# First output tile on one Trainium2 core: products with the low weights behind those with the high ones, and VectorE's three low parts behind the last head's P

## The chip, the cores and the metric

The kernel runs on one core of a Trainium2 chip. The metric is the device time of one execution in microseconds (us); of several executions the median counts. A comparison is called same when it lies within 0.2% (2.8 us here).

## The reference

The input x has 8 rows (batches) of 512 tokens with 1024 values, all float32. Two blocks follow each other:

```
x = x + layernorm(attention(layernorm(x)))      # 8 heads of 64, w_qkv (1536 x 1024), w_o (1024 x 512)
x = x + layernorm(ffn(layernorm(x)))            # W (1024 x 1024), b, and a low-rank part:
ffn(h) = h @ W.T + b + (h @ A[:r].T) @ B[:, :r].T   # r of 8, 16, 32, 64, chosen per token by the gate's largest score
attention: scores = k q^T, masked scores -10000, softmax over the key axis, times v, then w_o
```

## The kernel before

**Products in three passes.** Every float32 product is made of three TensorE products: an operand is split into a high part (rounded to the fast float32 form) and a low part (the rest), and high x high, high x low and low x high are added in PSUM. ScalarE makes the high parts (an ACTIVATE with Copy), VectorE or GpSimd the low parts (a subtraction of the high part from the raw one). For the FFN the weights W, A and the gate lie side by side in `wag`, 8 chunks (k = 0 to 7) of 128 x 1092: raw `wag_raw`, high `wagh`, low `wagl`. The activations are `x2Th` and `x2Tl`.

**Two phases.** `attention_phase` walks over the 8 rows of x: projections, then for each of 8 heads (h) the scores, their softmax `pr` (the P of a head; GpSimd normalises it in `normalise`, four tensor_scalar over 512, 384, 256 and 128 columns), the transposes of P into `ps_t` in three groups g = 0, 1, 2 (`transpose_p`), high and low parts of the transposed P (`p_hi` on ScalarE, `p_lo` on VectorE) and the values (`values`). `output_phase` walks over 32 tiles of 128 tokens: output product, layernorm, FFN (`ffn`), layernorm. Between them stands `last_body`, the attention of row 7, in which every engine's order is written out by hand: it already loads and splits the output phase's weights (`next_high`, `next_low`) and carries the first tiles through their output product (`tile_out` copies its PSUM halves out), residual (`tile_residual`), layernorm (`tile_scale`, `tile_norm`, `tile_statistics`) and transposes (`tile_high`, `tile_low`: the high and low parts of x2 of tile 0).

**What sets the order.** Each engine runs its own queue in order. Between engines there are only counting semaphores, waited for with `wait_ge`. Those that matter here: `next_lo` counts VectorE's low parts (three of w_o, then wag[4], wag[5], wag[6], so 4, 5, 6 of the table `LOW_READY` plus one mean these), `next_lo_pool` those of GpSimd (w_o 3, wag[0] to wag[3], wag[7]); `x2_lo` counts the halves of `tile_low`; `us_ready` tells that the routing of tile 0 (`route` on VectorE) is done, after which TensorE transposes `us`.

**The first FFN tile.** `ffn` makes three PSUM banks in the order 2, 0, 1. Per bank and chunk k it issues high x high, high x low weight, low x high weight. Into the first bank of tile 0 it puts the rest of the attention phase: after k = 1 `last_transposes` (the third group of the last head's P) and after k = 4 `last_values` (the last head's values).

```python
LOW_READY = {4: KV, 5: KV + 1, 6: KV + 2}

next_low(W.wag[4])        # VectorE, last_body
next_low(W.wag[5])
tile_low()
p_lo(7, 0, b)
p_lo(7, 1, b)
vals_sum(6, b)
p_lo(7, 2, b)
next_low(W.wag[6])
product_statistics(2)
vals_sum(7, b)
tile_statistics(1)
```

GpSimd's own end of `last_body`, which the change leaves as it is, reads: weights and normalise of head 7, diagonal, `tile_scale(0, 1, 1)`, `next_low(W.wag[7])`, `tile_residual(1)` (two additions of 128 x 512), `tile_scale(1, 4, 1)`, `tile_scale(0, 2, 2)`.

Of the kernel before, what the change touches and what calls it, by code (L numbers as in the profile page):

```python
# [33 lines left out]
class Output:  # L34
# [3 lines left out]
    def __init__(self, nc, ctx, whole, S, D, PART, R, NAG):  # L38
        def sb(name, shape, dt, c=ctx):
            return c.enter_context(nc.sbuf_tensor(name, shape, dt))  # L40

        def sem(name):
            return whole.enter_context(nc.semaphore(name))

        KD, KV = D // P, PART // P
        self.R, self.KV = R, KV

        self.woh = sb("woh", [P, KV, D], F32R)
        with ExitStack() as early:
            wo_raw = sb("wo_raw", [P, KV, D], F32, early)  # L50
        self.wol = sb("wol", [P, KV, D], F32R)
        self.vraw = sb("vraw", [P, 2, KV, P], F32)
        self.vh = sb("vh", [P, 2, KV, P], F32R)
        self.vl = sb("vl", [P, 2, KV, P], F32R)

        self.wagh = sb("wagh", [P, KD, NAG], F32R)
        self.bo_s = sb("bo_s", [P, D], F32)
        with ExitStack() as early:
            wag_raw = sb("wag_raw", [P, KD, NAG], F32, early)
            B_raw = sb("B_raw", [P, D], F32, early)  # L60
        self.wagl = sb("wagl", [P, KD, NAG], F32R)
        self.Bl = sb("Bl", [P, D], F32R)
        self.Bh = sb("Bh", [P, D], F32R)
        self.y = [sb(f"y{i}", [P, D], F32) for i in range(3)]
        used = 2 * KD * NAG + 2 * D + D + 3 * D
        small = sb("small", [P, 2 * KD * (2 * PART + S) - used - P], F32)
        self.uT = sb("uT", [P, P], F32R)

        with ExitStack() as early:
            self.z = sb("z", [P, D], F32, early)  # L70
            self.xs = [sb("xt0", [P, D], F32, early)]
        self.plane4 = [sb("plane4h", [P, 2, PART], F32R), sb("plane4l", [P, 2, PART], F32R)]
        self.spare = small[:, 128:128 + PART]
        self.stats_2 = small[:, 72:84]

        self.x1 = [sb("x1_0", [P, D], F32), self.y[0]]
        self.x2Th = [sb("x2Th0", [P, KD, P], F32R)]
        self.x2Tl = [sb("x2Tl0", [P, KD, P], F32R)]
        self.x2n = sb("x2n", [P, D], F32)
        self.floats = 2 * KV * D + 6 * PART + 2 * KD * (2 * PART + S) + 6 * D  # L80

        self.stats = [small[:, 12 * c:12 * c + 12] for c in range(3)]
        row = [[36 + 5 * i + j for j in range(5)] for i in range(6)]
        self.mv = [small[:, r[0]:r[0] + 2] for r in row]
        self.var_eps = [small[:, r[2]:r[2] + 1] for r in row]
        self.rstd = [small[:, r[3]:r[3] + 1] for r in row]
        self.shift = [small[:, r[4]:r[4] + 1] for r in row]
        self.gb_s = small[:, 66:70]

        self.chunks = [("wo", k, wo_raw[:, k, :], self.woh[:, k, :], self.wol[:, k, :]) for k in range(KV)]  # L90
        self.chunks += [("wag", k, wag_raw[:, k, :], self.wagh[:, k, :], self.wagl[:, k, :]) for k in range(KD)]
        self.chunks += [("B", 0, B_raw[:, :], self.Bh[:, :], self.Bl[:, :])]
        self.wag, self.B = range(KV, KV + KD), KV + KD

        self.next_lo = sem("next_lo")
        self.next_lo_pool = sem("next_lo_pool")
        self.bo_landed = sem("bo_landed")
        self.gb_landed = sem("gb_landed")
        self.v_landed = [sem(f"v_landed{i}") for i in range(2)]
        self.x_landed = [sem(f"xt_landed{i}") for i in range(2)]  # L100
        self.v_hi = sem("v_hi")
        self.v_ready = sem("v_ready")
        self.o_full = sem("o_full")
        self.y_done = sem("y_done")
        self.mv_ready = [sem(f"mv_ready{i}") for i in range(3)]
        self.ln_ready = [sem(f"ln_ready{i}") for i in range(3)]
        self.z_done = sem("z_done")
        self.x1_done = sem("x1_done")
        self.x2n_ready = sem("x2n_ready")
        self.x2_full = sem("x2_full")  # L110
        self.x2_hi = sem("x2_hi")
        self.x2_lo = sem("x2_lo")
        self.zf_done = sem("zf_done")
        self.out_done = sem("out_done")
        self.f_done = sem("f_done")
        self.out_stored = [sem(f"out_stored{i}") for i in range(2)]
        self.m_full = sem("m_full")
        self.m_out = sem("m_out")
# [7 lines left out]
def attention_phase(nc, whole, x, wqkvT, bqk, bv, valsT, wl_late, vals_stored, ps_o, C, W, woT, bo, wagT, BT, gb):  # L126
# [58 lines left out]
    with ExitStack() as ctx:  # L185
# [3 lines left out]
        def sem(name):  # L189
            return whole.enter_context(nc.semaphore(name))  # L190
# [109 lines left out]
        vlo_done = sem("vlo_done")  # L300
        vals_ready = sem("vals_ready")
        next_landed = [sem(f"next_landed{n}") for n in range(len(W.chunks))]
        next_hi = sem("next_hi")
        next_lo, next_lo_pool = W.next_lo, W.next_lo_pool

        HIGH_ROWS = [PT[:, PT_OFF[j]:PT_OFF[j] + (NT - j) * P] for j in range(NT)]
# [383 lines left out]
        def vector(dve):  # L690
# [243 lines left out]
            def last_body(b):  # L934
# [47 lines left out]
                tile_out(0, 1)  # L982
                p_lo(4, 0, b)
                p_lo(4, 1, b)
                vals_sum(3, b)
                reciprocal(5, b)
                tile_vals_low(2)
                p_lo(4, 2, b)

                scores_max(6, b)  # L990
                tile_out(1, 0)
# [15 lines left out]
                p_lo(6, 2, b)  # L1007
                reciprocal(7, b)

                next_low(W.wag[4])  # L1010
                next_low(W.wag[5])
                tile_low()
                p_lo(7, 0, b)
                p_lo(7, 1, b)
                vals_sum(6, b)
                p_lo(7, 2, b)
                next_low(W.wag[6])
                product_statistics(2)
                vals_sum(7, b)
# [675 lines left out]
def output_phase(nc, whole, x, valsT, vals_stored, ps_o, C, W, woT, bf, out):  # L1695
# [19 lines left out]
    with ExitStack() as ctx:  # L1715
# [3 lines left out]
        def sem(name):  # L1719
            return whole.enter_context(nc.semaphore(name))  # L1720
# [597 lines left out]
        def tensor(pe, last_transposes, last_values):  # L2318
# [74 lines left out]
            def low_rank(banks):  # L2393
                for g in banks:
# [3 lines left out]
                                         stop=(Bp is Bl), skip_group_check=True)  # L2398
                    last.then_inc(f_full, 1)

            def ffn(b, i, last_tiles, first_tiles):
                first = first_tiles and i == 0
                n = 4 * b + i
                xh, xl = x2Th[i % 2], x2Tl[i % 2]
                pe.wait_ge(x2_lo, 2 * n + 2)
                pe.wait_ge(next_lo_pool, 5)
                for m, g in enumerate(BANK_ORDER):
                    cols = slice(GW * g, GW * g + GW)

                    pe.wait_ge(f_done, 3 * n + m + 1)  # L2410
                    for k in range(KD):
                        if m == 0 and k in LOW_READY:
                            pe.wait_ge(next_lo, LOW_READY[k])
                        elif m == 0 and k == KD - 1:
                            pe.wait_ge(next_lo_pool, 6)
                        for a, w in ((xh, wagh), (xh, wagl), (xl, wagh)):
                            last = pe.matmul(ps_f[:, g, 0:GW], a[:, k, :], w[:, k, cols],  # L2417
                                             start=(k == 0 and a is xh and w is wagh), stop=False,
                                             skip_group_check=True)
                        if first and g == 2 and k == 1:  # L2420
                            last_transposes(pe)
                        if first and g == 2 and k == KD // 2:
                            last_values(pe)
                        if g == 1 and k == (0 if last_tiles else KD - 3):

                            pe.wait_ge(us_ready, n + 1)
                            if not first_tiles:
                                pe.wait_ge(m_out, 7 * pair_count(b, 0 if last_tiles else i) + (11 if i % 2 and not last_tiles else 7))
                            pe.transpose(ps_u[:, 0:P].bitcast(F32R), us[:, :].bitcast(F32R), ident_r[:, :])\
                                .then_inc(ut_full, 1)  # L2430
                            if not last_tiles:
                                transpose_x2(n + 1)
                        if g == 1 and k == KD // 2 - 1 and last_tiles:

                            pe.wait_ge(ut_ready, n + 1)
                            low_rank(BANK_ORDER[:2])
                    if g == 2:
                        last.then_inc(u_full, 1)
                        if i % 2 and not first_tiles and not last_tiles:
                            pair_third(b, i)  # L2440
                    if g == 0 and last_tiles and i < 3:
                        transpose_x2(n + 1)

                if last_tiles:
                    low_rank(BANK_ORDER[2:])
                else:
                    pe.wait_ge(ut_ready, n + 1)
                    pe.wait_ge(next_lo, KV + 3)
                    low_rank(BANK_ORDER)
# [86 lines left out]
```

## Time and profile before

| | us |
|---|---|
| median of 3 executions | 1416.1 (1415.28 to 1416.1) |
| the profiled execution | 1415.63 |
| its span (first to last instruction) | 1413.8 |
| TensorE busy | 1396.7 |
| VectorE busy | 1045.6 |
| GpSimd busy | 709.0 |
| ScalarE busy | 693.3 |

The profiled execution took 1.83 us more than its span; that part lies outside of the instructions. In the rows PE is TensorE, DVE VectorE, ACT ScalarE, POOL GpSimd. Matmuls overlap, so TensorE's pace is read from the distance of their starts, not from their durations. The end of attention and the first FFN tile lie between 800 and 850 us of the span.

### The profile page before, as it was taken

The numbers are of one execution on the slowest core, as the hardware profiler recorded it, in microseconds if no ns is written. First come the engines' busy times: TensorE is split into PE (matmuls) and PEld (weight loads), VectorE is DVE, ScalarE is ACT, GpSimd is POOL, SyncE is SP. The second block draws the span as 40 slices with busy tenths as digits, with TensorE's granted clock in tenths as the row PEclk, the third lists the DMA queues.
The fourth block names the chain that finished last, engine by engine and source line by source line (L and its number), as shares of the span: only waits on it lengthen the run. The fifth ranks groups of instructions, "written<-read, shape, count | busy, mean of one in ns | idle before, by whom it ended". The sixth has DMA issues, their size and how long they took to land.

```text
span 1413.8 us, 25005 instructions
## 1 busy us (share of the span) xinstructions
PE 1396.7 (99%) x7796; PEld 1249.2 (88%) x7796; DVE 1045.6 (74%) x2204; ACT 693.3 (49%) x1498; POOL 709.0 (50%) x1268
## 2 busy tenths in 40 slices
PE   7999999999999999999999999999999999999998
PEld 6888888888888888888888889999999999999998
DVE  7676685776775776766756888898878787878764
ACT  6365465564573664654654863433333333333332
POOL 3364462572562563644624785555555555555542
PEclk9999999999999999999999999999999999999999
DMA  7334334224233243342332643232222222222311
GB/s 253 127 98 121 113 93 148 89 97 139 97 111 108 94 139 111 96 122 111 95 102 93 213 145 109 105 105 92 102 89 104 104 103 89 91 92 99 119 75 60
DMA packets 68773, 157.54 MB, mean 111 GB/s; under 512 B 7424, under 2 KB 31232, under 8 KB 68736
## 3 DMA queue, kind: packets, MB, share of 16 engines
q1 hardware_dynamic: 68736, 157.08, 33.3%
q8 instruction: 19, 0.31, 0.1%
q14 instruction: 18, 0.15, 0.0%
HBM read 62.15 MB, written 25.69 MB: 62 GB/s over the span
## 4 chain that ended last, share of the span: by engine, by line
PE 89%; POOL 4%; issue 3%; POOLq 1%; DVE 1%; ACT 1%; DVEq 1%; DMA 0%; SPq 0%; ACTq 0%
PE ps_f L2417 23%; PE ps_o L1483 21%; PE ps_o L1514 12%; PE ps_s L1534 6%; PE ps_o L2336 6%; PE ps_v L1358 5%; PE ps_t L1396 3%; PE ps_o L1477 3%; PE ps_z L2336 2%; PE ps_f L2397 2%; PE ps_o L1437 2%; PE ps_x L2387 1%; PE ps_v L1366 1%; POOL wagl L609 1%; PE ps_o L1495 1%
## 5 line engine op out<-in xcount | busy, mean ns | idle before, releaser
L2417 PE MATMUL ps_f<-wagh,x2Th 128*128 128x364 f32 x768 | 254.7, 332 | 0.0
L2417 PE MATMUL ps_f<-wagh,x2Tl 128*128 128x364 f32 x768 | 252.5, 329 | 0.0
L2417 PE MATMUL ps_f<-wagl,x2Th 128*128 128x364 f32 x768 | 252.1, 328 | 0.0
L1483 PE MATMUL ps_o<-xTh,wh 128*128 128x512 f32 x424 | 172.2, 406 | 0.0
L572 POOL TENSOR_SCALAR pr<-pr,nwm,rden 128x512 f32<-128x512 f32 (+3 forms) x256 | 161.0, 644 | 11.3 <-issue 11.3
L1483 PE MATMUL ps_o<-xTh,wl 128*128 128x512 f32 x424 | 166.1, 392 | 0.0
L1483 PE MATMUL ps_o<-xTl,wh 128*128 128x512 f32 x424 | 165.4, 390 | 0.0
L548 POOL TENSOR_TENSOR cw<-wm,cnt 128x4 f32<-128x4 f32 x64 | 12.8, 201 | 301.1 <-ACT pr L1122 301.1
L2417 PEld LDWEIGHTS ps_f<-wagh,x2Th 128*128 128x128 f32 x768 | 144.2, 188 | 1.9 <-DVE f L2117 0.2
L2417 PEld LDWEIGHTS ps_f<-wagl,x2Th 128*128 128x128 f32 x768 | 144.5, 188 | 1.6
L2417 PEld LDWEIGHTS ps_f<-wagh,x2Tl 128*128 128x128 f32 x768 | 144.4, 188 | 0.0
L724 DVE TENSOR_TENSOR PT<-ps_t,PT 128x512 fp32r<-128x512 f32 (+1 forms) x192 | 110.5, 598 | 36.8 <-ACT PT L1079 32.5
L1122 ACT ACTIVATE pr<-ps_s,nm 128x128 f32<-128x128 f32 (+3 forms) x256 | 131.0, 524 | 0.2
L1079 ACT ACTIVATE PT<-ps_t 128x512 fp32r<-128x512 f32 (+1 forms) x192 | 95.2, 530 | 57.2 <-PE ps_t L1396 50.6
L1881 POOL TENSOR_TENSOR small<-small,eps 128x1 f32<-128x1 f32 x90 | 20.9, 232 | 198.8 <-DVE small L1961 184.3
L786 DVE TENSOR_REDUCE nm<-ps_s 128x1 f32<-128x129 f32 (+3 forms) x256 | 108.0, 484 | 2.2
L1514 PE MATMUL ps_o<-wh_v,xTh 128*128 128x512 f32 x256 | 100.5, 393 | 0.0
L1514 PE MATMUL ps_o<-wh_v,xTl 128*128 128x512 f32 x256 | 99.8, 390 | 0.0
L1483 PEld LDWEIGHTS ps_o<-xTh,wl 128*128 128x128 f32 x424 | 79.6, 188 | 17.9
L1534 PE MATMUL ps_s<-kst,qst 128*128 128x128 f32 (+3 forms) x512 | 94.2, 326 | 0.0
L2207 ACT ACTIVATE f<-f,small 128x512 f32<-128x512 f32 x62 | 47.2, 809 | 95.2 <-POOL small L1885 95.2
L1358 PEld LDWEIGHTS ps_v<-PT,v 128*128 128x128 f32 x512 | 83.5, 188 | 9.6 <-issue 1.4
(303 smaller groups left out, 3425.4 us busy)
## 6 DMA issues: line engine op xcount, KB each, us to landing
p_words<-pr SPq DMA_DIRECT2D x56, 448.0 KB, 2.8
kst<-kst SPq DMA_DIRECT2D x64, 256.0 KB, 3.7
x<-in_x SPq DMA_DIRECT2D x31, 512.0 KB, 3.4
x2r<-x2n SPq DMA_DIRECT2D x30, 512.0 KB, 2.9
xs<-in_x SPq DMA_DIRECT2D x24, 512.0 KB, 4.4
out<-x SPq DMA_DIRECT2D x23, 512.0 KB, 2.6
p_words<-pr SPq DMA_DIRECT2D x56, 192.0 KB, 2.3
valsT<-vt SPq DMA_DIRECT2D x64, 128.0 KB, 2.3
```

The costliest lines, as they stand in the source:

```text
L572: done = pool.tensor_scalar(at, at, nwm[:, q, i:i + 1], rden[:, q, i:i + 1], ALU.add, ALU.mult)
L724: dve.tensor_tensor(LOW_GROUPS[g].rearrange("p (n c) -> p n c", n=n), ps_t[g % 2][:, 0:n * P].rearrange("p (n c) -> p n c", n=n), HIGH_GRO ...
L786: last = dve.tensor_reduce(nm[:, q, i:i + 1], ps_s[:, lo:hi], AX.X, ALU.max, negate=True)
L1079: act.activation(HIGH_GROUPS[g], ps_t[g % 2][:, 0:n * P].rearrange("p (n c) -> p n c", n=n), ACT.Copy)\
L1122: last = act.activation(pr[:, q, S_OFF[i]:S_OFF[i] + n], ps_s[:, PS_OFF[i]:PS_OFF[i] + n], ACT.Exp, bias=nm[:, q, i:i + 1], accum_out=acc[ ...
L1358: pe.matmul(ps_v[:, j * P:], v[:, j, h, :], rows, start=(j == 0 and rows is HIGH_ROWS[0]), stop=False, skip_group_check=True)
L1483: done = pe.matmul(ps[:, :], w[:, k, c:c + P], xT[:, k, :], start=(k == 0 and w is wh and xT is xTh), stop=(k == KD - 1 and w is wl), skip ...
L1514: done = pe.matmul(ps_j[t % 2][:, :], xT[:, k, t * P:(t + 1) * P], w, start=(k == 0 and xT is xTh and w is w_high), stop=(k == KD - 1 and ...
L1534: last = pe.matmul(ps_s[:, PS_OFF[i]:PS_OFF[i] + (i + 1) * P], qst[p % 2][:, s, i * P:(i + 1) * P], kst[p % 2][:, s, part, 0:(i + 1) * P], ...
L2207: return act.activation(out_, in_, ACT.Identity, scale=rstd[r], bias=shift[r])
L2336: last = pe.matmul(bank, a[:, room, k, :], w[part][:, k, :], start=(start and k == 0 and a is rooms_h and part == 0), stop=(stop and k == ...
L2417: last = pe.matmul(ps_f[:, g, 0:GW], a[:, k, :], w[:, k, cols], start=(k == 0 and a is xh and w is wagh), stop=False, skip_group_check=True)
```

## The change

TensorE: the first bank of tile 0 gets a function of its own, `first_ffn`. It issues all sixteen products with `wagh` first (high and low activations), with `last_transposes` after k = 2 and `last_values` behind them, then the products with `wagl` for k = 0 to 5, then the eight products with `wagh` for k = 0 to 3 of the second bank, then `wagl` for k = 6 and 7 of the first, then `wagl` for k = 0 to 3 of the second. The loop of `ffn` goes on with k = 4 of the second bank. The number and the shapes of the products stay the same. `next_hi` becomes a semaphore that this function can wait for. VectorE: `next_low` of wag[4] and wag[5] moves from before `tile_low` to behind `p_lo(7, 2)`, in front of that of wag[6]. Three heads earlier, `reciprocal(5)` moves before `vals_sum(3)`, and `p_lo(4, 2)` before `tile_vals_low(2)`.

```diff
@@ VectorE, last_body, between head 4 and head 5
                 p_lo(4, 1, b)
+                reciprocal(5, b)
                 vals_sum(3, b)
-                reciprocal(5, b)
+                p_lo(4, 2, b)
                 tile_vals_low(2)
-                p_lo(4, 2, b)
@@ VectorE, last_body, head 7
-                next_low(W.wag[4])
-                next_low(W.wag[5])
                 tile_low()
                 p_lo(7, 0, b)
                 p_lo(7, 1, b)
                 vals_sum(6, b)
                 p_lo(7, 2, b)
+                next_low(W.wag[4])
+                next_low(W.wag[5])
                 next_low(W.wag[6])
@@ TensorE, output phase
+            def first_ffn():
+                xh, xl = x2Th[0], x2Tl[0]
+
+                def add(g, k, a, w):
+                    return pe.matmul(ps_f[:, g, 0:GW], a[:, k, :], w[:, k, GW * g:GW * g + GW],
+                                     start=(k == 0 and a is xh and w is wagh), stop=False, skip_group_check=True)
+
+                pe.wait_ge(x2_lo, 2)
+                pe.wait_ge(W.next_hi, W.wag[KD - 1] + 1)
+                pe.wait_ge(f_done, 1)
+                for k in range(KD):
+                    add(2, k, xh, wagh)
+                    add(2, k, xl, wagh)
+                    if k == 2:
+                        last_transposes(pe)
+                last_values(pe)
+                pe.wait_ge(next_lo_pool, 5)
+                for k in range(KD - 2):
+                    if k in LOW_READY:
+                        pe.wait_ge(next_lo, LOW_READY[k])
+                    add(2, k, xh, wagl)
+                second = BANK_ORDER[1]
+                pe.wait_ge(f_done, 2)
+                for k in range(KD // 2):
+                    add(second, k, xh, wagh)
+                    add(second, k, xl, wagh)
+                pe.wait_ge(next_lo, LOW_READY[6])
+                add(2, 6, xh, wagl)
+                pe.wait_ge(next_lo_pool, 6)
+                add(2, 7, xh, wagl).then_inc(u_full, 1)
+                for k in range(KD // 2):
+                    add(second, k, xh, wagl)
```

VectorE's queue around the last head. `wagl<-wag_raw,wagh` is `next_low`, `x2Tl` is `tile_low`, `PT<-ps_t,PT` is `p_lo`, `vt<-ps_v` is `vals_sum`. Before:

```order
L795 RECIPROCAL rden<-den 128x4
L808 TENSOR_TENSOR wagl<-wag_raw,wagh 128x1092 x2
L846 TENSOR_TENSOR x2Tl<-ps_s,x2Th 128x512 x2
L724 TENSOR_TENSOR PT<-ps_t,PT 128x512 x2
L802 SCALAR_TENSOR_TENSOR vt<-ps_v,bv_s,vt 64x512
L724 TENSOR_TENSOR PT<-ps_t,PT 128x256
L808 TENSOR_TENSOR wagl<-wag_raw,wagh 128x1092
L839 BN_STATS small<-y 128x6 x2
```

And of the change:

```order
L796 RECIPROCAL rden<-den 128x4
L847 TENSOR_TENSOR x2Tl<-ps_s,x2Th 128x512 x2
L725 TENSOR_TENSOR PT<-ps_t,PT 128x512 x2
L803 SCALAR_TENSOR_TENSOR vt<-ps_v,bv_s,vt 64x512
L725 TENSOR_TENSOR PT<-ps_t,PT 128x256
L809 TENSOR_TENSOR wagl<-wag_raw,wagh 128x1092 x3
L840 BN_STATS small<-y 128x6 x2
```

The three subtractions now stand in one row; two of them left the place right behind the reciprocal.

TensorE's queue behind the last product of the attention phase. `ps_t<-ident,pr` are the transposes of P, `ps_f` the FFN's products. Before:

```order
L1553 MATMUL ps_o<-woh,vl 128x512
L1398 MATMUL ps_t<-ident,pr 128x128 x8
L2417 MATMUL ps_f<-wagh,x2Th 128x364
L2417 MATMUL ps_f<-wagl,x2Th 128x364
L2417 MATMUL ps_f<-wagh,x2Tl 128x364
```

Of the change, the same place and then the end of the last head's values:

```order
L1554 MATMUL ps_o<-woh,vl 128x512
L1399 MATMUL ps_t<-ident,pr 128x128 x8
L2406 MATMUL ps_f<-wagh,x2Th 128x364
L2406 MATMUL ps_f<-wagh,x2Tl 128x364
```

```order
L1367 MATMUL ps_v<-PT,totals 128x384
L2406 MATMUL ps_f<-wagl,x2Th 128x364 x6
L2406 MATMUL ps_f<-wagh,x2Th 128x364
L2406 MATMUL ps_f<-wagh,x2Tl 128x364
```

The low weights moved out of the triples: the first row of six is k = 0 to 5 of the first bank, and a second row of six (k = 6 and 7 of the first bank, k = 0 to 3 of the second) stands eight `wagh` products later.

VectorE's queue three heads earlier; `vl<-vraw,vh` is `tile_vals_low(2)`, and the last row opens the scores of head 6. Before:

```order
L802 SCALAR_TENSOR_TENSOR vt<-ps_v,bv_s,vt 64x512
L795 RECIPROCAL rden<-den 128x4
L812 TENSOR_TENSOR vl<-vraw,vh 128x512
L724 TENSOR_TENSOR PT<-ps_t,PT 128x256
L773 MEMSET hold 1x1
```

And of the change:

```order
L796 RECIPROCAL rden<-den 128x4
L803 SCALAR_TENSOR_TENSOR vt<-ps_v,bv_s,vt 64x512
L725 TENSOR_TENSOR PT<-ps_t,PT 128x256
L813 TENSOR_TENSOR vl<-vraw,vh 128x512
L774 MEMSET hold 1x1
```

The reciprocal moved in front of the sum, and the subtraction behind the low part of P.

## Rows read from the trace of the kernel before

**Rows 1.** Waits of TensorE: us in total, times, longest.

```profile
PE ps_t L1398 <- POOL pr L572: 1.3, 1, 1.3
```

**Rows 2.** Busy time by stretch: length, then PE, PEld, DVE, ACT, POOL, clock, DMA.

```profile
860.00:1413.00 553.00, 546.73 (x3203) 521.32 (x3201) 439.56 (x1003) 202.05 (x334) 282.86 (x426) 1.00 0.27 95
```

**Rows 3.** Timeline of TensorE: start, us, engine, line, what [idle before].

```profile
827.20 1.09 PE L1398 MATMUL ps_t<-ident,pr 128*128 128x128 f32 x8 [1.27 <-POOL pr L572]
828.05 0.41 PE L2417 MATMUL ps_f<-wagh,x2Th 128*128 128x364 f32 x1
...
829.27 0.44 PE L1398 MATMUL ps_t<-ident,pr 128*128 128x128 f32 x2
...
832.65 0.33 PE L2417 MATMUL ps_f<-wagh,x2Th 128*128 128x364 f32 x1
...
835.14 0.33 PE L2417 MATMUL ps_f<-wagh,x2Th 128*128 128x364 f32 x1
...
841.12 0.22 PE L2429 MATMUL ps_z<-ident_words,us 128*128 128x128 f32 x1
...
849.49 0.33 PE L2417 MATMUL ps_f<-wagh,x2Th 128*128 128x364 f32 x1
```

**Rows 4.** Timeline of GpSimd, columns as before.

```profile
803.92 2.40 POOL L572 TENSOR_SCALAR pr<-pr,nwm,rden 128x512 f32<-128x512 f32 x4 [0.18 <-issue]
...
811.65 0.20 POOL L556 TENSOR_TENSOR wn<-wm,rden 128x4 fp32r<-128x4 f32 x1
...
822.58 1.16 POOL L556 TENSOR_TENSOR wn<-wm,rden 128x4 fp32r<-128x4 f32 x1
823.91 3.23 POOL L572 TENSOR_SCALAR pr<-pr,nwm,rden 128x512 f32<-128x512 f32 x4 [0.17 <-issue]
...
829.17 2.55 POOL L609 TENSOR_TENSOR wagl<-wag_raw,wagh 128x1092 fp32r<-128x1092 f32 x1
```

**Rows 5.** Timeline of VectorE from the last reciprocal to tile 1.

```profile
822.41 2.47 DVE L808 TENSOR_TENSOR wagl<-wag_raw,wagh 128x1092 fp32r<-128x1092 f32 x2
825.59 1.29 DVE L846 TENSOR_TENSOR x2Tl<-ps_s,x2Th 128x512 fp32r<-128x512 f32 x2 [0.71 <-ACT x2Th L1156]
...
830.96 1.92 DVE L808 TENSOR_TENSOR wagl<-wag_raw,wagh 128x1092 fp32r<-128x1092 f32 x1
...
839.16 0.25 DVE L1996 TENSOR_TENSOR us<-um,us 128x64 fp32r<-128x64 f32 x1
...
845.54 1.24 DVE L2008 TENSOR_TENSOR x2Tl<-ps_x,x2Th 128x512 fp32r<-128x512 f32 x2
```

**Rows 6.** Timelines of single GpSimd and VectorE instructions that overlap.

```profile
812.38 0.96 DVE L812 TENSOR_TENSOR vl<-vraw,vh 128x512 fp32r<-128x512 f32 x1
...
812.78 1.10 POOL L572 TENSOR_SCALAR pr<-pr,nwm,rden 128x384 f32<-128x384 f32 x1
...
831.68 2.35 POOL L625 TENSOR_TENSOR y<-xt,z 128x512 f32<-128x512 f32 x1
...
833.99 1.29 POOL L625 TENSOR_TENSOR y<-xt,z 128x512 f32<-128x512 f32 x1
```

**Rows 7.** Timeline of ScalarE.

```profile
822.55 1.52 ACT L1150 ACTIVATE x2n<-x,small 128x512 f32<-128x512 f32 x2 [0.60 <-POOL small L617]
...
830.02 1.51 ACT L1150 ACTIVATE z<-y,small 128x512 f32<-128x512 f32 x2
```

**Rows 8.** Timeline of VectorE three heads earlier, and one row of its later copies.

```profile
802.00 0.74 DVE L802 SCALAR_TENSOR_TENSOR vt<-ps_v,bv_s,vt 64x512 f32<-64x512 f32 x1 [0.47 <-DMA valsT<-vt]
802.93 0.18 DVE L795 RECIPROCAL rden<-den 128x4 f32<-128x4 f32 x1 [0.20 <-POOL den L550]
...
804.03 0.62 DVE L777 COPY_PREDICATED_SCALAR ps_s<-maskf,masked 128x384 f32 x1
...
816.10 1.28 DVE L821 TENSOR_TENSOR y<-ps_o,bo_s 128x512 f32<-128x512 f32 x2
```

**Rows 9.** TensorE's product that needs the first of these copies.

```profile
817.34 0.48 PE L1553 MATMUL ps_o<-woh,vh 128*128 128x512 f32 x1
```

More of the change, by code:

```diff
@@ L93, in __init__ @@
         self.wag, self.B = range(KV, KV + KD), KV + KD
+        self.next_hi = sem("next_hi")
         self.next_lo = sem("next_lo")
@@ L302, in attention_phase @@
         next_landed = [sem(f"next_landed{n}") for n in range(len(W.chunks))]
-        next_hi = sem("next_hi")
+        next_hi = W.next_hi
         next_lo, next_lo_pool = W.next_lo, W.next_lo_pool
@@ L2404, in ffn @@
                 xh, xl = x2Th[i % 2], x2Tl[i % 2]
-                pe.wait_ge(x2_lo, 2 * n + 2)
-                pe.wait_ge(next_lo_pool, 5)
+                if first:
+                    first_ffn()
+                else:
+                    pe.wait_ge(x2_lo, 2 * n + 2)
                 for m, g in enumerate(BANK_ORDER):
+                    if first and m == 0:
+                        continue
                     cols = slice(GW * g, GW * g + GW)
[L2410 to L2415, printed above, removed]
+                    if not first or m > 1:
+                        pe.wait_ge(f_done, 3 * n + m + 1)
+                    for k in range(KD // 2 if first and m == 1 else 0, KD):
                         for a, w in ((xh, wagh), (xh, wagl), (xl, wagh)):
@@ L2419, in ffn @@
                                              skip_group_check=True)
[L2420 to L2423, printed above, removed]
                         if g == 1 and k == (0 if last_tiles else KD - 3):
```

## The prediction

> **What bounds the kernel now.** I read the list of waits first, because TensorE is busy in nearly the whole span: in the part before the last head it names one wait worth a name, 1.3 us of TensorE behind `pr` of GpSimd [rows 1]. The table of stretches then says what a shift is worth: from 860 to 1413 us TensorE is busy 546.73 of 553 us [rows 2], so what the first FFN tile gains or loses is carried to the end, microsecond for microsecond. The timeline of TensorE shows where: transposes of the last head's P start at 827.20 after 1.27 us of idle, the first FFN product at 828.05, and the second piece of `last_transposes` at 829.27. Fifteen FFN products are issued when the row at 832.65 starts, thirty at 835.14: that is 2.49 us for 15, so 0.166 us a product and no wait among them [rows 3].
>
> Why P is late is in GpSimd's timeline. Its small instruction `wn` takes 0.20 us at 811.65 but 1.16 at 822.58, and the four pieces of `pr` take 2.40 us at 803.92 but 3.23 at 823.91 [rows 4]. In just this time VectorE runs the two low parts of wag[4] and wag[5], 822.41 to 824.88 [rows 5]. Both engines read their operands from SBUF there, and one stops the other: `wn` ends at 823.74, where VectorE's first one ends.
>
> The same happens the other way: VectorE's third low part, issued at 830.96, takes 1.92 us and ends at 832.88 [rows 5]; GpSimd's low part of wag[7] ends at 831.72 [rows 4], so 1.15 us of work stand behind it. GpSimd's first addition, issued at 831.68, takes 2.35 us and ends at 834.03 [rows 6], 1.16 us behind VectorE's end. So they take turns, whole instruction by whole instruction. That a waiting one is let in before the other engine's next is shown at 812.38: VectorE's subtraction waits for one piece of `pr` and takes 0.96 us, and the next piece, issued at 812.78, then takes 1.10 [rows 6].
>
> The Trainium skill has this as "SBUF — State Buffer", section "SBUF: two separate sides": the port pair that VectorE and GpSimd share is an exclusive lock held for a whole instruction, taken by a VectorE instruction with two SBUF inputs against GpSimd's reads. The trace agrees (1.16 for 0.20 us). The page does not say who comes next when both wait; under the even sharing that it argues against, my sum below would be about 0.3 us higher, since the second low part would come 1.2 us later and the third at the same time.
>
> **The change part by part.**
>
> *1. The two low parts leave the place behind the reciprocal.* `wn` would start at 822.58 as before and take 0.20, the issue gap is 0.18 and `pr` takes 2.40: it ends at 825.36, where it now ends at 823.91 + 3.23 = 827.14. That is 1.78 us earlier, before TensorE asks (827.20 - 1.27 = 825.93) [rows 3, 4]. So the wait of 1.27 us goes. What is late next is x2: `tile_low` ends at 825.59 + 1.29 = 826.88 and hangs on ScalarE [rows 5], which hangs on GpSimd's `tile_scale` [rows 7]; moving the low parts does nothing for it. The transposes take 828.05 - 827.20 = 0.85 us and end at 826.78, so TensorE would wait a little for x2.
>
> *2. Three heads earlier.* The reciprocal starts at 802.93 because GpSimd's denominator comes then, and the sum of the values, which now starts at 802.00 and takes 0.74 us, would stand behind it [rows 8]. So would the low part of P, and `tile_vals_low(2)` would meet GpSimd's `pr`, that starts 0.35 earlier. I get 0.84 us later for the scores of head 6 (now 804.03) and 0.25 for GpSimd, that waits once for 0.6 us and has got 0.35 before. Waits of VectorE for the next heads take up most of the 0.84. GpSimd runs on without idle to the last head, so its 0.25 stays: `pr` of head 7 ends at 825.61, x2 is ready at 827.13. Estimate for this part: 0.25 on the path, 0 if GpSimd recovers, 0.5 if TensorE also waits for a copy of `tile_out`: the two that start at 816.10 take 1.28 us together, so the first is there at about 816.8, and the product at 817.34 needs it [rows 8, 9], a slack of 0.5 us for a delay of up to 0.84.
>
> *3. TensorE up to the low weights.* The first FFN product starts at 827.17 in place of 828.05, 0.88 us earlier. Six products (1.00 us, 0.08 for the change of form) reach `last_transposes` at 828.25. P's low part there follows the transposes by the same distance as before, so it is ready; before, TensorE stood still for 0.14 (829.27 - 828.05 - 1.08) [rows 3]. Then 0.19, ten products in 1.74, the values in 1.55: 831.73. Sixteen products are done by then, and before fifteen by 832.65 [rows 3], so without further waits TensorE is 0.92 + 0.17 = 1.09 us ahead. This is the gain.
>
> *4. The three low parts come as one block.* `p_lo(7, 2)` ends 1.27 us earlier than before with the transposes, so VectorE asks for the first one at 830.96 - 1.27 = 829.69 [rows 5]. GpSimd's wag[7] ended at 829.17 + 2.55 = 831.72 and moves by -1.78 + 0.25, to 830.19 [rows 4]. VectorE waits for it. Then GpSimd has its two additions ready, since z comes from ScalarE, whose row at 830.02 moves with P too [rows 7]. By turns: wag[4] ends at 830.19 + 1.15 = 831.34, addition 832.50, wag[5] 833.65, addition 834.81, wag[6] 835.96. TensorE wants wag[4] at 831.73 + 4 x 0.166 = 832.4 (there), wag[5] at 832.6 (waits until 833.7), and after that product and eight others, at 835.2, wag[6]: it waits until 836.0. Thirty products are done then too, in place of 835.14 [rows 3]: **+0.86 us**. The eight products put between cover 1.33 of the 2.31 us between wag[5] and wag[6].
>
> *5. What is queued behind them on VectorE.* Statistics, the last head's sum, statistics of tile 1 and the routing: the last instruction of the routing ends at 839.16 + 0.25 = 839.41, 6.53 us behind the end of wag[6] (832.88) [rows 5]. This comes to 842.49. TensorE asks for it in the third bank, before at 841.12 [rows 3] and now at 841.98: it waits to 842.55, another **0.57**. At `tile_low`'s successor for tile 1, which ended at 846.78 [rows 5], VectorE is late by 3.08: 849.86, and TensorE needs it at 849.49 + 1.43 = 850.92 [rows 3]. Here the delay is used up.
>
> Sum: 0.86 + 0.57 = +1.43 us. Against its own time, 1415.63, this is 1417.1; the median of the runs shown is 1416.1, 0.47 higher, which makes 1417.5. I take the middle, 1417.3. No difference below 2.8 us (0.2%) can be told from none by a measurement of this kernel, so this is "same".
>
> **The rivals.**
>
> *A. The three low parts run back to back.* For it: at 822.41 two of them took 2.47 us together with only a tiny instruction of GpSimd between. Against it: GpSimd's next there, `pr`, came 0.2 us too late for the turn. Then wag[5] and wag[6] end at 832.5 and 833.6, TensorE meets no wait, and the routing (840.2) is behind TensorE (841.12 - 1.09 = 840.03) by 0.2: -0.9 us, 1415.0.
>
> *B. One turn fewer.* If GpSimd has just one addition before wag[6] (z later than I think, or its first one ahead of wag[4] hiding behind VectorE's own wait), wag[6] ends at 834.80: thirty products at -0.3, routing 841.33 against 840.8, in all +0.3: 1416.2. The change then moves nothing, gain and loss being equal.
>
> *C. Slower by more than 0.2%.* The block of three meets a further GpSimd instruction: each turn is 1.16 us. wag[6] ends at 837.1, thirty products are at +2.0, the routing wait brings it to +2.6. VectorE is then 4.24 late and the x2 of tile 1 ends at 851.02, its PSUM copies right behind it are needed by the same tile, so some 0.5 us are lost there too: +3.1, 1418.9. It decides only from 1.4 us of delay beyond my sum on. Against it: GpSimd has no third long instruction there.
>
> *D. Faster by more than 0.2%.* Nothing in the trace holds it: all TensorE idle in this stretch is under 1.8 us.
>
> **How the numbers follow.** Forecast 0.5; A 0.25; B 0.17; C 0.06; D 0.02. The forecast gives the time. From A's 1415.0 less 0.4 for the spread of the runs before (1415.28 to 1416.1) to 1417.5 with part 2 at its worse end and half a turn more gives 1414.6 to 1418.6; C and D are left out. Faster by over 0.2%: 0.02; within: 0.92; slower: 0.06.
>
> **What would show it.** The wait of 1.27 us for `pr` is gone and `wn` takes 0.20: part 1. A short wait for x2 before the first FFN product: part 1's "next". The three low parts take 4.8 us or more between their ends and lie between the two additions: part 4; if they lie side by side, A. Two waits of TensorE for `wagl`, of about 1.1 and 0.8 us, and one of about 0.6 for `us`: parts 4 and 5. The prediction is wrong if TensorE waits for none of these, or if a wait appears behind 850 us.

## The result and the profile after

The change makes the kernel slower by a little: 1417.88 us in the median of 22 executions, against 1416.11 us of the kernel before (22 executions), a ratio of 1.0012 with a 95% interval of 1.0007 to 1.0018. That is 1.8 us (1.0 to 2.5 by the interval), within the 0.2% that counts as same, though the interval leaves out zero. The profiled execution has a span of 1415.6 us (before 1413.8). The forecast was 1417.3 us, +1.4 on the trace.

Waits of TensorE in the span after, from 780 to 860 us:

```profile
PE ps_f L2406 <- DVE wagl L809: 1.6, 2, 1.1
PE ps_z L2460 <- DVE us L1997: 0.3, 1, 0.3
```

The wait for `pr` of [rows 1] is gone, and in its place TensorE waits for VectorE's low parts (twice, 1.6 us in sum) and for the routing. The timeline of GpSimd after, against [rows 4], shows that the cause named for the old wait was right:

```profile
822.70 0.20 POOL L557 TENSOR_TENSOR wn<-wm,rden 128x4 fp32r<-128x4 f32 x1
823.08 2.37 POOL L573 TENSOR_SCALAR pr<-pr,nwm,rden 128x512 f32<-128x512 f32 x4 [0.17 <-issue]
```

`wn` takes 0.20 us in place of 1.16, the four pieces of `pr` 2.37 in place of 3.23: P is there at 825.45, 1.69 us earlier. The timeline of TensorE, against [rows 3]:

```profile
827.04 0.44 PE L2406 MATMUL ps_f<-wagh,x2Th 128*128 128x364 f32 x1
...
828.15 0.38 PE L1399 MATMUL ps_t<-ident,pr 128*128 128x128 f32 x2
...
831.46 1.00 PE L2406 MATMUL ps_f<-wagl,x2Th 128*128 128x364 f32 x5
833.54 0.43 PE L2406 MATMUL ps_f<-wagl,x2Th 128*128 128x364 f32 x1 [1.08 <-DVE wagl L809]
...
835.84 1.27 PE L2406 MATMUL ps_f<-wagl,x2Th 128*128 128x364 f32 x6 [0.53 <-DVE wagl L809]
...
842.37 0.28 PE L2460 MATMUL ps_z<-ident_words,us 128*128 128x128 f32 x1 [0.26 <-DVE us L1997]
...
850.93 0.33 PE L2452 MATMUL ps_f<-wagh,x2Th 128*128 128x364 f32 x1
```

The first FFN product starts 1.01 us earlier (828.05 before). At 831.46 sixteen products are behind TensorE, and before, fifteen were at 832.65. Then it stands still for wag[5] and, eight products later, for wag[6]: the thirty-first product starts at 835.84, 0.70 us behind the kernel before. The wait for `us` makes it 1.25, and tile 1 starts 1.44 us late.

Single instructions of VectorE and GpSimd after, in narrow windows, show what holds the low parts up:

```profile
829.60 1.59 DVE L809 TENSOR_TENSOR wagl<-wag_raw,wagh 128x1092 fp32r<-128x1092 f32 x1
827.47 2.56 POOL L610 TENSOR_TENSOR wagl<-wag_raw,wagh 128x1092 fp32r<-128x1092 f32 x1
829.99 2.33 POOL L626 TENSOR_TENSOR y<-xt,z 128x512 f32<-128x512 f32 x1
...
831.11 2.37 DVE L809 TENSOR_TENSOR wagl<-wag_raw,wagh 128x1092 fp32r<-128x1092 f32 x1
...
832.29 2.34 POOL L626 TENSOR_TENSOR y<-xt,z 128x512 f32<-128x512 f32 x1
...
833.41 2.38 DVE L809 TENSOR_TENSOR wagl<-wag_raw,wagh 128x1092 fp32r<-128x1092 f32 x1
```

Read the ends (start plus duration): GpSimd 830.03, VectorE 831.19, GpSimd 832.32, VectorE 833.48, GpSimd 834.63, VectorE 835.79. Each comes 1.13 to 1.16 us behind the other engine's, and the rows of the last four last about twice that (2.33 to 2.38 us): half of each is waiting for the other engine, which the profile counts as busy.

### The profile page after: what moved, and what is told of

Read it like the earlier page. It is cut to its first block, busy times and chain, and to the rows that moved or that the text cites. A ratio compares the mean times of both kernels' runs of the same rounds, so it can differ in the third digit from the quotient of the medians.

```text
span 1415.6 us, 24981 instructions
## 1 busy us (share of the span) xinstructions
PE 1398.2 (99%) x7796; PEld 1249.7 (88%) x7796; DVE 1048.3 (74%) x2204; ACT 692.6 (49%) x1498; POOL 706.1 (50%) x1268
## 4 chain that ended last, share of the span: by engine, by line
PE 88%; POOL 4%; issue 3%; DVE 1%; POOLq 1%; ACT 1%; DMA 1%; DVEq 1%; ACTq 0%
PE ps_f L2452 23%; PE ps_o L1484 21%; PE ps_o L1515 12%; PE ps_s L1535 6%; PE ps_o L2337 6%; PE ps_v L1359 5%; PE ps_t L1397 3%; PE ps_o L1478 3%; PE ps_z L2337 2%; PE ps_f L2398 2%; PE ps_o L1438 2%; PE ps_x L2388 1%; PE ps_v L1367 1%; POOL wagl L610 1%; PE ps_t L1484 1%
## 5 line engine op out<-in xcount | busy, mean ns | idle before, releaser
L2452 PE MATMUL ps_f<-wagh,x2Th 128*128 128x364 f32 x756 | 250.8, 332 | 0.0
L2452 PE MATMUL ps_f<-wagh,x2Tl 128*128 128x364 f32 x756 | 248.7, 329 | 0.0
L2452 PE MATMUL ps_f<-wagl,x2Th 128*128 128x364 f32 x756 | 248.3, 328 | 0.0
```

## The experiments

Executions of one kernel differ by some tenths of a microsecond before the part in question is reached, so besides the span I give **the rest**: from the start of the first product of the output phase (`tile_product`, near 789.5) to the end of the span. Before 624.37 us, after 626.19: +1.82. The differences are taken before rounding, so the last digit can differ from that of the rounded spans and starts.

| kernel | thirty-first FFN product | span | rest, against before | median (the kernel before, measured beside it) | ratio, 95% interval |
|---|---|---|---|---|---|
| the change | 835.84 | 1415.61 | +1.82 | 1417.88 (1416.11) | 1.0012 [1.0007, 1.0018] |
| 1 low parts back | 835.91 | 1414.70 | +0.14 | 1415.35 (1416.33) | 0.9992 [0.9983, 1.0001] |
| 2 low parts moved alone | 837.65 | 1416.27 | +2.57 | 1418.85 (1416.33) | 1.0017 [1.0008, 1.0026] |
| 3 GpSimd's additions later | 833.92 | 1413.31 | -0.35 | 1415.41 (1416.33) | 0.9996 [0.9987, 1.0005] |
| 4 without the reordering at head 5 | 835.99 | 1415.79 | +2.16 | 1417.59 (1416.33) | 1.0011 [1.0002, 1.0020] |
| 5 that reordering alone | 835.30 | 1413.97 | +0.15 | 1415.91 (1416.60) | 0.9997 [0.9988, 1.0006] |
| 6 as 3, without the reordering | 836.86 | 1416.34 | +2.33 | 1415.69 (1416.60) | 0.9994 [0.9985, 1.0003] |
| 7 one GpSimd addition more | 837.49 | 1417.27 | +2.92 | 1419.13 (1416.60) | 1.0016 [1.0007, 1.0025] |
| 8 as 3, again | 834.22 | 1413.58 | -0.36 | 1415.37 (1416.60) | 0.9992 [0.9983, 1.0001] |

The medians of the experiments have intervals of about 1.3 us to either side. They tell the change and experiments 2, 4 and 7 from the kernel before, but do not rank the others: experiment 1, with a rest of +0.14, has a median 0.98 us below the kernel before, and experiment 3, with -0.35, one 0.92 below. What follows rests on the traces, one execution each; experiments 3 and 8 are the same kernel and repeat the rest to 0.01 us.

The theory: the two engines take turns at something that only one of them can have, and the change puts three of VectorE's instructions where GpSimd has two that alternate with them. Its rivals: TensorE's new order costs by itself; or three such subtractions in a row are slow by themselves.

**1. The two low parts back in their old place, TensorE's new order kept.**

```diff
+                next_low(W.wag[4])
+                next_low(W.wag[5])
                 tile_low()
                 p_lo(7, 0, b)
                 p_lo(7, 1, b)
                 vals_sum(6, b)
                 p_lo(7, 2, b)
-                next_low(W.wag[4])
-                next_low(W.wag[5])
                 next_low(W.wag[6])
```

> The changed kernel, with VectorE's low parts of wag[4] and wag[5] back in their old place behind the last reciprocal. Theory (turns): GpSimd's wn takes 1.16 us again and TensorE waits about 1.3 us for pr before the last transposes; the third low part stands alone and ends near 833.0, so TensorE waits for no wagl in its new order, and reaches its thirty-first FFN product within 0.2 us of the kernel before (835.1). Span as before, 1413.6 to 1414.1 us, 1.5 to 1.8 less than the change. Rival (the new order of TensorE's products costs by itself): the thirty-first product stands 0.5 us or more later than 835.1 and the span stays at 1414.5 or above.

The rest is 0.14 us over the kernel before, and the wait for P is back. The timelines of this kernel:

```profile
828.12 1.09 PE L1399 MATMUL ps_t<-ident,pr 128*128 128x128 f32 x8 [1.26 <-POOL pr L573]
...
823.50 1.15 POOL L557 TENSOR_TENSOR wn<-wm,rden 128x4 fp32r<-128x4 f32 x1
824.83 3.23 POOL L573 TENSOR_SCALAR pr<-pr,nwm,rden 128x512 f32<-128x512 f32 x4 [0.17 <-issue]
```

In absolute times both signs of the rival came: the thirty-first product stands 0.77 us later than in the kernel before, and the span is 1414.7, not 1414.1 at most. But the first output product is already 0.73 later (790.19 against 789.46), and this part of the run has nothing of the change in it; the profiled execution (1416.5 us) was the slowest of its eleven. From the first output product on, the thirty-first comes 0.04 us later than before, and in experiment 5, which has the same reordering at head 5 in TensorE's old order, 0.17; the rest is +0.14 in one and +0.15 in the other. So the new order costs nothing by itself, and where the low parts are early it gains nothing over the rest.

**2. Only the move of the two low parts, in TensorE's old order** (in the kernel before, the VectorE lines of the change at the last head and nothing else).

> The kernel before, with nothing changed but the place of the low parts of wag[4] and wag[5], which stand behind p_lo(7, 2) in front of that of wag[6]. Theory (turns): the low parts end near 831.1, 833.4 and 835.7 as in the change; with TensorE's old order (high, low, high per chunk) it wants wag[4] at its thirteenth product, near 829, and waits about 2.2 us, then some 0.3 to 0.8 for wag[5] and 1.8 to 2.0 for wag[6]: thirty products at about 837.7 to 838, and the span 2.5 to 3.2 us over the kernel before. Rival (the low parts are not what TensorE waits for, the new order is): span within 0.5 us of the kernel before, or under that of the change (1415.6).

```profile
830.96 0.43 PE L2417 MATMUL ps_f<-wagh,x2Th 128*128 128x364 f32 x1 [1.75 <-DVE wagl L808]
...
835.55 0.43 PE L2417 MATMUL ps_f<-wagh,x2Th 128*128 128x364 f32 x1 [1.52 <-DVE wagl L808]
```

TensorE waits 3.3 us in place of 1.6, and the rest is +2.57, without the 0.15 us of the reordering that experiment 5 measures. So the new order is worth 0.9 us where the low parts are late (2.57 + 0.15 - 1.82): it is the half of the change that pays for part of the other. All three waits are shorter than expected (1.75 and 1.52 us for about 2.2 and 1.8 to 2.0), and the span, +2.4, lies just under the 2.5 expected. The one for wag[5] is too short for the list, 0.23 us by the starts of the products around it: the last head's values stand between wag[4] and wag[5] in the old order and cover most of it.

**3 and 8. GpSimd's two additions wait for the three low parts.**

```diff
                 next_low(W.wag[7])
+                pool.wait_ge(W.next_lo, W.KV + 2)
                 tile_residual(1)
```

> The changed kernel, with one wait added: GpSimd's two additions of tile_residual(1) wait until VectorE's three low parts are done. Theory (turns): the three low parts then take 1.2 us each and end near 831.2, 832.4 and 833.5 in place of 831.2, 833.5, 835.8; TensorE waits for none of them and for us at most 0.4 us; its thirty-first product stands near 834.1 and the span is 1412.9 to 1413.4, 0.5 to 0.9 below the kernel before and 2.2 to 2.7 below the change. Rival (the three low parts are slow by themselves, because they stand in a row or because of TensorE's reads): they stay at 2.3 us each, TensorE waits the same 1.1 and 0.5 us, and with the additions later the span is 1415.6 or above.

> The changed kernel with GpSimd's additions behind the three low parts once more, since its first comparison did not tell it from the kernel before. Theory: from the product at 789 to the one near 1375 it takes 585.9 to 586.1 us against 586.4 before, so the median is 0.3 to 0.9 us below that of the kernel before. Rival: the gain was the jitter of that run, and it takes 586.3 or more.

Timelines of the second of the two, first VectorE, then GpSimd:

```profile
829.76 4.00 DVE L810 TENSOR_TENSOR wagl<-wag_raw,wagh 128x1092 fp32r<-128x1092 f32 x3
...
833.84 2.54 POOL L626 TENSOR_TENSOR y<-xt,z 128x512 f32<-128x512 f32 x2 [3.64 <-DVE wagl L810]
```

The three take 4.00 us, of which the first waits 0.4 for GpSimd's wag[7], in place of 6.19 us; the two additions take 2.54 in place of 4.63. TensorE waits for no `wagl` and none of the first tile's waits is left in the list. Nothing else was changed, so both rivals fall: standing in a row and TensorE's order are the same here. The rest is 624.01 and 624.00 us, 0.35 and 0.36 below the kernel before, where 0.5 to 0.9 was expected for the span. The thirty-first product is 1.06 us ahead in experiment 3 (833.92 for 835.14, less 0.16 for its earlier first output product), so some 0.7 us are given back behind it, about 0.4 of them in tile 0. The later additions are not the reason there: the third low part still ends later than before (833.76 in experiment 8, before 832.88), VectorE runs without a pause from it to the routing, which ends 6.52 us behind it (before 6.53), and TensorE, which is ahead, starts the transposes of `us` 0.06 us after the routing ends (840.28 and 840.34), a wait too short for the list. ScalarE's `uT` follows in the same way: it ends at 842.36, and the product that reads it starts at 842.41; in the kernel before, 1.4 us lay between the two.

By the medians the two runs are 0.9 and 1.2 us below the kernel before, but their intervals reach to 1.0005 and 1.0001, and experiments 1 and 6 lie as low: faster than the change, yes; faster than the kernel before by the traces only.

**4. The change without its reordering at head 5.**

> The changed kernel without its reordering three heads earlier (the sum before the reciprocal, the low values before the low part of P again). Theory: that reordering costs 0.1 to 0.2 us of the path: the products at 808.15 and 817.56 stand at 808.0 and 817.3 again, everything behind them 0.1 to 0.2 us earlier, span 1415.4 to 1415.6. Rival: it is worth something (it shortens GpSimd's wn of head 5), and without it the span is 1415.8 or above.

It went the rival's way in the trace: the rest is 0.34 us longer than with the reordering, and TensorE waits for x2:

```profile
827.33 0.44 PE L2406 MATMUL ps_f<-wagh,x2Th 128*128 128x364 f32 x1 [0.56 <-DVE x2Tl L847]
```

VectorE's timeline of this kernel says why:

```profile
802.61 0.74 DVE L803 SCALAR_TENSOR_TENSOR vt<-ps_v,bv_s,vt 64x512 f32<-64x512 f32 x1 [1.28 <-DMA valsT<-vt]
803.39 0.18 DVE L796 RECIPROCAL rden<-den 128x4 f32<-128x4 f32 x1
```

In [rows 8] the sum waits 0.47 us for a DMA (the store of an earlier head's values) and starts at 802.00, and the reciprocal behind it is on time for GpSimd. Here the DMA lands later, the reciprocal with it, and GpSimd's whole queue up to the last head (`wn` of head 7 starts at 822.87, with the reordering at 822.70). The comparison is a fair one: in the profiled execution of the change the same store lands at 802.38, here at 802.52, before at 801.91. The medians do not show a gain: without the reordering the kernel is 1.3 us over the kernel before, with it 1.8, and the intervals overlap widely.

**5. The reordering alone, on the kernel before.**

> The kernel before, with only the reordering three heads earlier. Seen by now: the sum of the values there waits for a DMA whose landing differs from run to run (it started at 801.4, 802.0 and 802.6), and the reciprocal stood behind it. Theory: with the reciprocal in front, GpSimd's wn takes 0.20 us and starts at about 803.1 in each run; the scores of head 6 come 0.8 us later, TensorE's products near 808.1 and 817.5 are 0.1 to 0.3 us later, and the wait for pr at 827 takes up all of it: span within 0.2 us of the kernel before. Rival (it pays by itself): TensorE's wait for pr is shorter than 1.0 us and the span 0.3 us or more below the kernel before.

The rest is +0.15, and the span within the 0.2 us expected: this is the price of the reordering against an execution in which the DMA is early. I had expected the wait for `pr` to take it up. It does not: the transposes behind that wait start 0.16 us later (827.36, before 827.20) and the wait is 1.25 us as before, so the P of the last head is late by as much.

**6. GpSimd's additions later, without the reordering.**

> The changed kernel with GpSimd's additions behind the three low parts, and without the reordering three heads earlier. Theory: low parts 1.2 us each, no wait of TensorE for wagl; the wait for x2 before the first FFN product is 0.1 to 0.6 us, by where the DMA of the values lands. Measured from the product at 789 to the one near 1375, 585.9 to 586.6 us (before 586.4, with the reordering 586.0). Rival (the reordering costs, as forecast): under 585.9.

Missed, by a DMA that landed later still in the profiled execution, a size for which nothing was forecast. VectorE's and TensorE's timelines:

```profile
805.17 0.74 DVE L804 SCALAR_TENSOR_TENSOR vt<-ps_v,bv_s,vt 64x512 f32<-64x512 f32 x1 [2.49 <-DMA valsT<-vt]
805.95 0.18 DVE L797 RECIPROCAL rden<-den 128x4 f32<-128x4 f32 x1
...
807.10 1.50 PE L1360 MATMUL ps_v<-PT,v 128*128 128x512 f32 x8 [0.93 <-DVE PT L726]
809.38 1.09 PE L1400 MATMUL ps_t<-ident,pr 128*128 128x128 f32 x8 [0.57 <-POOL pr L573]
```

That one execution lost about 2 us there; its other executions did not, the median is 1415.69. So its rest tells nothing of the additions, and much of the reordering; the three low parts take 4.17 us here, as short as in experiment 8.

**7. One more GpSimd addition in front of `tile_residual(1)`, of double width.**

```diff
                 next_low(W.wag[7])
+                pool.wait_ge(W.x_landed[0], 32)
+                pool.wait_ge(W.z_done, 6)
+                pool.tensor_tensor(W.x1[1][:, :], W.xs[0][:, :], W.z[:, :], ALU.add)
+                pool.drain()
                 tile_residual(1)
```

> The changed kernel with one more GpSimd addition of 128 x 1024 in front of tile_residual(1), which writes what the two additions write again. Theory (turns): it takes the first turn of GpSimd and holds VectorE 2.4 us in place of 1.2: low parts end near 831.2, 834.8 and 837.1; TensorE waits 2.3 us for wag[5] and 0.5 for wag[6], reaches its thirty-first product near 837.1, waits again for us, and VectorE is late by 4.4 us in tile 0, so that TensorE also waits 0.3 to 0.8 us in front of or in tile 1: span 1416.9 to 1417.8, 1.3 to 2.2 over the change. Rival (the engines share evenly, or GpSimd's queue has no part in it): low parts end within 0.5 us of 835.8 and the span is that of the change, 1415.6, within 0.4.

```profile
835.19 0.43 PE L2410 MATMUL ps_f<-wagl,x2Th 128*128 128x364 f32 x1 [2.16 <-DVE wagl L813]
837.49 1.27 PE L2410 MATMUL ps_f<-wagl,x2Th 128*128 128x364 f32 x6 [0.54 <-DVE wagl L813]
```

The low parts end at 831.76, 835.14 and 837.44 (expected 831.2, 834.8, 837.1, in a run that is 0.56 late at the first output product), the wait for wag[5] doubles, and the rest is 1.10 us over the change. The lower end of what was expected, 1.3, was missed: the third low part ends 1.09 us later than in the change (both from the first output product), TensorE's wait for `us` did not grow (0.26 us), so only the turn itself is paid, and no wait in tile 1.

## Why the prediction was right

It named the mechanism and the places in tile 0, and the time lies 0.6 us from the median measured. Against the kernel before it was low: +1.43 us on the trace, where the spans differ by 1.78 (the rest by 1.82), and the difference lies in places that it did not name. Its sentence that no difference below 2.8 us can be told from none does not hold either: with 22 executions of each kernel the interval is 1.0 to 2.5 us.

*Part 1 held.* P comes 1.69 us earlier (forecast 1.78, less 0.25 for part 2) and the next thing late is x2, as said: it ends at 826.99, and TensorE starts the FFN at 827.04, 0.13 before the forecast.

*Part 2 was right in size for the usual case and incomplete.* It took 0.25 us for GpSimd's delay; `wn` of the last head starts 0.12 later (822.70), experiment 5 shows 0.15 on the whole. TensorE itself loses 0.15 us too (from the first output product), at the output product at 808.15 (before 808.05) and not at the one near 817 that the prediction named. That it also takes GpSimd out from behind a DMA whose landing varies by more than 3 us between executions, I did not see, though [rows 8] name the DMA.

*Part 3 held.* Without the waits TensorE would be 1.09 us ahead by the forecast; in experiment 3, where they are gone, it is 1.06.

*Part 4 was the step that decided, and held to 0.2 us.* The low parts end at 831.19, 833.48 and 835.79, forecast 831.34, 833.65 and 835.96. The waits are 1.08 and 0.53 us (1.1 and 0.8), thirty products are +0.70 in place of +0.86. (The sign "4.8 us or more between their ends" was set too high by the prediction's own sum, 831.34 to 835.96; measured are 4.60.) Experiment 3 takes the turns away and 7 makes one longer; both move the low parts as the theory has it. The Trainium skill states in "SBUF — State Buffer", section "SBUF: two separate sides", that the pair of ports which the two engines share is locked for a whole instruction and not split between them. The six ends agree: an instruction waits for a whole one of the other engine and then takes 1.13 to 1.16 us. That the one that waits comes next, before the other engine's queue goes on, is what these runs add.

*Part 5 held for tile 0 and failed behind it.* TensorE loses 0.55 us between the thirty-first product and the transposes of `us` (forecast 0.57), of which the list shows 0.26 as a wait. Tile 1 starts +1.44, forecast +1.43. That this agrees to 0.01 is partly luck: at `us` TensorE is +1.25 where +1.43 was forecast, and it loses 0.19 more before tile 1, which the forecast did not have. ScalarE's `uT`, queued behind its `y`, ends at 844.38, and the product that reads it starts at 844.43.

The ten traces show what sets tile 1. In the change and in experiments 3, 4, 6, 7 and 8 the product that reads `uT` starts 0.05 us behind it, and the first FFN product of tile 1 starts 15.1 to 15.2 us behind the end of the third low part (835.79 and 850.93 in the change), whatever TensorE waited for on the way. In the kernel before and in experiments 1, 2 and 5 these distances are 1.4 us and 16.5 to 16.6. So in the first six TensorE follows the chain that begins with the end of that low part, and by this its two waits for `wagl` add nothing to the time of the change. This is read from the traces; no run took these two waits away and left the third low part as late.

But the sentence "Here the delay is used up" is wrong, and by the prediction's own words ("or if a wait appears behind 850 us") this is where its account fails: the rest is +1.82. TensorE loses 0.16 us more at the start of tile 2 and 0.13 near 918 us, at its transposes of `us`, in waits too short for the list. The rows, first before, then after:

```profile
868.46 0.39 PE L2327 MATMUL ps_o<-woh,vl 128*128 128x512 f32 x1
868.68 0.33 PE L2417 MATMUL ps_f<-wagh,x2Th 128*128 128x364 f32 x1
...
918.05 0.22 PE L2429 MATMUL ps_z<-ident_words,us 128*128 128x128 f32 x1
918.18 0.88 PE L2387 MATMUL ps_x<-ident_words,x2r 128*128 128x128 f32 x8
```

```profile
869.90 0.39 PE L2328 MATMUL ps_o<-woh,vl 128*128 128x512 f32 x1
870.21 0.40 PE L2452 MATMUL ps_f<-wagh,x2Th 128*128 128x364 f32 x1
...
919.70 0.28 PE L2460 MATMUL ps_z<-ident_words,us 128*128 128x128 f32 x1
919.91 0.87 PE L2388 MATMUL ps_x<-ident_words,x2r 128*128 128x128 f32 x8
```

The starts are 0.31 us apart where they were 0.22, and 0.21 where they were 0.13. Losses at the same two places stand in the traces of experiments 3, 4, 6, 7 and 8, and not in those of 1, 2 and 5. In the first five, as in the change, VectorE's `x2Tl` of tile 1 ends 1.3 us ahead of TensorE's first FFN product of tile 1, in the last three 2.6 to 2.7, as before: VectorE is later against TensorE. That fits, but no run tested it, and which semaphore ends these waits stays open.

Rival A (the three back to back, -0.9) did not occur by itself. Experiment 3 enforces it: TensorE is 0.90 us ahead at the transposes of `us`, as the rival has it, and then gives back all but 0.35. Rival B (one turn fewer) did not occur: both additions lie between the low parts. Rival C's price for a turn, 1.16 us, was right (1.10 in experiment 7), its loss in tile 1 did not come there.

## What to carry to other kernels

When an instruction is moved away from a place where it blocks another engine, look up what that other engine does at the new place: here VectorE's low parts left the way of `pr` and landed between GpSimd's additions, and the gain of 1.0 us became a loss of 1.8. VectorE's three subtractions, each with two SBUF inputs, took 6.19 us beside two additions of GpSimd and 4.00 with the additions behind them, and one wait that lets the needed block run first gave back 2.2 us of the rest. And an instruction that another engine waits for should not stand behind one that waits for a DMA, even if the profile at hand shows the DMA in time: this cost 0.3 us in the trace of experiment 4 and about 2 in that of experiment 6, too little or too seldom to show in a median.

## What I had not expected of the hardware

The landing of one DMA of 128 KB, the store of a head's values for which the sum waits, differs by almost 4 us between executions in which TensorE is within 0.4 us at the same place of its program (the first output product at 789.26 to 789.64):

| | issued | landed | the sum behind it starts | GB/s, share of 16 DMA engines, 795 to 807 us |
|---|---|---|---|---|
| experiment 2 | 794.05 | 801.33 | 801.44 | 377, 104.3% |
| before | 794.19 | 801.91 | 802.00 | 362, 103.0% |
| experiment 4 | 793.99 | 802.52 | 802.61 | 351, 103.2% |
| experiment 6 | 794.37 | 805.08 | 805.17 | 315, 100.8% |

The store is issued at nearly the same time in all four. In each of them it lands 0.35 to 0.43 us behind the last `wag_raw` chunk (546 KB) that was issued before it, and that chunk takes 10.5, 11.0, 11.7 and 13.2 us to land. So the small store comes in behind the bulk loads ahead of it, and what differs is how fast they go. The share of the DMA engines is hardly lower in experiment 6, where they move the least; why they do is open.
